# The last stage in seven tiles of 128 tokens instead of eight batches of 100, with the second attention's context re-laid by copies from DRAM to DRAM

## The reference, cut to what matters

```
x = x + L0_xattn(layernorm(x), ctx_512)      # 16 heads, causal
x = x + L0_ffn(layernorm(x))                 # 8 experts, top 2
x = x + L1_xattn(layernorm(x), ctx_512)      # 16 heads, latent context, rope
x = x + L1_ffn(layernorm(x))                 # int8-like quantised gate/up/down
```

```
ctx_c   = einsum('bhsl,bld->bhsd', attn, kv_rope)
ctx_lat = einsum('bhsd,hkd->bshk', ctx_c, w_kc_kv)
out     = ctx_lat.reshape(b, s, H * K) @ Wo.T
xq  = quant(x);  gate, up = split(xq @ quant(w_gate_up).T)
y   = quant(silu(gate) * up) @ quant(w_down).T
```

## Time and profile before

| | |
|---|---|
| median of 3 runs | 873.49 us (873.23 to 875.69) |
| the profiled execution's own time | 876.1 us |
| its span | 874.3 us |
| mean granted clock of TensorE | 0.925 |
| PE busy | 734.6 us (84%) |
| DVE busy | 522.6 us (60%) |
| ACT busy | 424.3 us (49%) |
| POOL busy | 254.4 us (29%) |
| DMA packets of the SP queue | 48605, 99.50 MB, 33.8% of 16 engines' time |

### The profile page before, as it was taken

One profiled execution on the slowest core, in us unless ns is written; L12 is line 12 of the kernel. 1 busy time (PEld: TensorE's weight loads), 2 busy tenths in 40 slices (PEclk: granted clock), 3 DMA queues, 4 the chain that ended last, 5 costly groups with the idle time before them and its releaser, 6 DMA issues.

```text
span 874.3 us, 13418 instructions
## 1 busy us (share of the span) xinstructions
PE 734.6 (84%) x4533; PEld 585.1 (67%) x4533; DVE 522.6 (60%) x1065; ACT 424.3 (49%) x790; POOL 254.4 (29%) x284
## 2 busy tenths in 40 slices
PE   0799988718999999795989989989886888999974
PEld 0597776617777777695878778778773455777752
DVE  4877675565666665255763664664663436777683
ACT  3523666255555554212664674663663314544552
POOL 1000931331122220522372461560640002222232
PEclk9997999758999999855999999999999799999997
DMA  8556632996665556952010110010015911110000
GB/s 260 189 179 220 234 105 84 351 330 230 206 212 168 181 172 203 296 116 69 1 37 23 35 46 24 22 46 24 25 39 225 339 58 48 60 57 10 10 19 19
DMA packets 51793, 108.71 MB, mean 124 GB/s; under 512 B 12149, under 2 KB 30321, under 8 KB 48953
## 3 DMA queue, kind: packets, MB, share of 16 engines
q1 hardware_dynamic: 48605, 99.50, 33.8%
q0 software_dynamic: 3136, 8.53, 4.1%
HBM read 88.59 MB, written 19.43 MB: 124 GB/s over the span
## 4 chain that ended last, share of the span: by engine, by line
PE 47%; issue 20%; DVE 12%; POOL 7%; DMA 6%; ACT 5%; SPq 1%; ACTq 1%; POOLq 0%; DVEq 0%
PE PS L148 10%; PE PS L150 9%; PE PS L149 9%; POOL wraw L759 4%; PE PS L1160 3%; PE PS L1505 3%; PE PS L1221 3%; DMA fq_raw<-foldq_in 2%; PE PS L1522 2%; ACT w_hi L811 2%; PE PS L1264 2%; DMA raw<-wkv_in 2%; DVE wscale L1760 1%; PE PS L1204 1%; DMA fp_raw<-foldp_in 1%
## 5 line engine op out<-in xcount | busy, mean ns | idle before, releaser
L759 POOL TENSOR_TENSOR wraw<-wraw,rinv 128x361 f32<-128x361 f32 (+1 forms) x104 | 80.7, 787 | 140.0 <-DVE rinv L1718 139.9
L1561 DVE TENSOR_TENSOR w_lo<-w,w_hi 128x1408 fp32r<-128x1408 f32 x40 | 64.9, 1623 | 38.6 <-ACT w_hi L811 38.6
L907 ACT ACTIVATE wraw<-PS,nmx 128x361 f32<-128x361 f32 (+1 forms) x104 | 58.6, 564 | 38.1 <-DVE nmx L1725 30.3
L1725 DVE TENSOR_REDUCE nmx<-PS 128x1 f32<-128x361 f32 (+1 forms) x104 | 55.0, 530 | 33.6 <-PE PS L150 33.6
L786 POOL TENSOR_TENSOR wraw<-gs,us 100x352 f32<-100x352 f32 x32 | 30.3, 947 | 153.4 <-ACT gs L1078 128.9
L711 POOL DMA_INDIRECT xb<-xn_scratch,rows x20 | 33.7, 1687 | 104.6 <-PE PS L1132 101.5
L811 ACT CAST w_hi<-w 128x1408 fp32r x40 | 54.7, 1369 | 16.8 <-issue 9.4
L148 PE MATMUL PS<-w_hi,xt_hi 128*128 128x352 f32 x160 | 57.0, 356 | 5.8 <-DVE xt_lo L1555 5.8
L148 PE MATMUL PS<-pf_hi,cx_hi 128*100 128x512 f32 x128 | 53.9, 421 | 8.9 <-DVE pf_lo L1896 3.7
L1728 DVE TENSOR_TENSOR pt_lo<-PS,pt_hi 128x384 fp32r<-128x384 f32 x96 | 52.3, 546 | 11.9 <-ACT pt_hi L913 11.1
L1320 PE MATMUL PS<-ident,wraw 128*128 128x128 f32 x312 | 52.0, 276 | 6.2 <-POOL wraw L759 3.4
(11 more groups left out here) (277 smaller groups left out, 2044.0 us busy)
## 6 DMA issues: line engine op xcount, KB each, us to landing
w<-w_in SPq DMA_DIRECT2D x20, 768.0 KB, 5.3
w<-w_in SPq DMA_DIRECT2D x8, 1408.0 KB, 11.5
fq_raw<-foldq_in SPq DMA_DIRECT2D x6, 1088.0 KB, 7.5
cx_raw<-ctx_scratch SPq DMA_DIRECT2D x8, 800.0 KB, 5.4
ctx_scratch<-ctxo SPq DMA_DIRECT2D x24, 256.0 KB, 2.0
ys_scratch<-yb SPq DMA_DIRECT2D x20, 256.0 KB
wraw<-wup_in SPq DMA_DIRECT2D x12, 256.0 KB, 4.4
w1q<-w_scratch SPq DMA_DIRECT2D x1, 2816.0 KB
```

The lines of the kernel that those rows point to most:

```text
L759: pool.tensor_tensor(P1[slot][0:rows, 0:NK], P1[slot][0:rows, 0:NK], rinv[0:rows, jj, t:t + 1].broadcast_to((rows, NK)), ALU.mult).then_in ...
L907: act.activation(P1[t % 8][r, 0:NK], PS[r, t % 4, 0:NK], ACT.Exp, bias=nmx[r, jj, t:t + 1], accum_out=rsum[r, jj, t:t + 1]).then_inc(C["ex ...
L1561: dve.tensor_tensor(WL[which][:, :], w12_of(dve_wlo.e, which), WH[which][:, :].bitcast(F32), ALU.subtract) \
L1725: dve.tensor_reduce(nmx[r, jj, t:t + 1], PS[r, t % 4, 0:NK], AX.X, ALU.max, negate=True).then_inc(C["max"], 1)
```

## The change

The last stage goes over NTT = 7 tiles of the 800 tokens in a row: six of 128 and one of 32. All its instructions take `tokens(n)` partitions or stationary columns in place of 100. Seven tiles need the residual and the context in that cutting:

- Residual: after the experts, SP stores X (eight DMAs of 100 rows) in `x_scratch` and loads it back in tiles (`XT`) when batch 6 of the second attention is under way. `XT` lies where X lay.
- Context: for each batch, a copy from `ctx_scratch[b]` to `tile_scratch` (DRAM to DRAM) puts the tokens in tile order. A tile's region is 128 partitions by 16 heads by tokens(n). A batch that a tile's bound cuts needs two pieces, so the eight batches are 14 pieces: 1, 2, 2, 2, 1, 2, 2, 2. Each run of contiguous bytes is one head's tokens of one piece: at most 400 bytes, and for batch 7 272 and 128. Batches 0 to 6 are copied four heads at a time, one batch later, each behind a store of the next batch; batch 7 is copied whole, after its own last store has landed.
- SP's order after that: foldp 2 and 3, load_ctx(0), foldp 4 to 7, load_ctx(1), the weights (their scale rows now for 128 partitions), load_ctx(2) and on.
- There is one buffer `CXR` in place of two: load_ctx(n) waits for `low_ctx(n - 1)`. It holds 2048 columns in place of 1600.
- The 11 transposes are split 7 and 4 over two banks in place of 6 and 5.

```
+NTT = -(-B * T // 128)
...
+        def tokens(n):
+
+            return min(128, B * T - 128 * n)
...
+        PIECES = []
+        for b in range(B):
+            cuts = sorted({b * T, (b + 1) * T} | {128 * n for n in range(NTT) if b * T < 128 * n < (b + 1) * T})
+            PIECES.append(list(zip(cuts[:-1], cuts[1:])))
...
+            for b in range(B):
+                sp.wait_ge(E["x"], TOPK * (b + 1))
+                sp.dma_start(x_scratch[b * T:(b + 1) * T], X[:, b, :]).then_inc(XSTORED, 16)
...
+            def move(b, heads, done):
+
+                h0, h1 = heads
+                for lo, hi in PIECES[b]:
+                    n = lo // 128
+                    r = tokens(n)
+                    tile = tile_scratch[:, 128 * NH0 * n:128 * NH0 * n + NH0 * r].rearrange("p (h t) -> p h t", h=NH0)
+                    batch = ctx_scratch[b].rearrange("p (h t) -> p h t", h=NH0)
+                    sp.dma_start(tile[:, h0:h1, lo - 128 * n:hi - 128 * n], batch[:, h0:h1, lo - b * T:hi - b * T]).then_inc(done, 16)
+
+            def stored(b):
+
+                sp.wait_ge(C["st0"], 16 * NG // 2 * (b + 1))
+                sp.wait_ge(C["st1"], 16 * NG // 2 * (b + 1))
+
+            for b in range(B):
+                if b + 2 < B:
+                    load_kv(b + 2, b % 2)
+                if b == B - 2:
+                    sp.wait_ge(XSTORED, 16 + 16 * B)
+                    sp.wait_ge(LN["xn"], 3 * B)
+                    full = B * T // 128
+                    sp.dma_start(XT[:, 0:full, :], x_scratch[0:128 * full].rearrange("(n p) d -> p n d", p=128)).then_inc(XLOADED, 16)
+                    sp.dma_start(XT[0:tokens(full), full, :], x_scratch[128 * full:B * T]).then_inc(XLOADED, 16)
+                if b > 0:
+                    stored(b - 1)
+                for g in range(NG):
+                    store_ctx(b, g)
+                    if b > 0:
+                        move(b - 1, (4 * g, 4 * g + 4), MOVED)
+            stored(B - 1)
+            move(B - 1, (0, NH0), MOVED_LAST)
+
+            def load_ctx(n):
+                if n == 0:
+                    sp.wait_ge(MOVED, 16 * NE + 16 * 4 * sum(len(PIECES[b]) for b in range(B - 1)))
+                if n == NTT - 2:
+                    sp.wait_ge(MOVED_LAST, 48 + 16 * len(PIECES[B - 1]))
+                wait(sp, O["cxl"], n)
+                sp.dma_start(of_tile(CXR, n), of_tile(tile_scratch[:, 128 * NH0 * n:B * ROWS], n)).then_inc(O[f"cx{n % 2}"], 16)
 
             load_foldp(2)
             load_foldp(3)
-            load_ctx(0, 0)
-            load_ctx(1, 1)
+            load_ctx(0)
             for i in range(4, NP1):
                 load_foldp(i)
+            load_ctx(1)
             sp.wait_ge(C["pv"], NG * B)
             sp.dma_start(W1Q[:, :, :], w1_scratch).then_inc(FFNW, 16)
...
+                r = tokens(n)
                 for h in heads:
-                    t = slice(h * T, (h + 1) * T)
-                    last = mm3(pe, PS[0:T, 6, :], CXH[j][:, t], CXL[j][:, t], PFH[:, h, :], PFL[:, h, :], h == 0, h == NH0 - 1)
+                    t = slice(h * r, (h + 1) * r)
+                    last = mm3(pe, PS[0:r, 6, :], CXH[j][:, t], CXL[j][:, t], PFH[:, h, :], PFL[:, h, :], h == 0, h == NH0 - 1)
...
-            for n in range(B):
+            for n in range(NTT):
                 pe_ffn(n, n % 2)
```

More of the change, by code:

```diff
@@ L321, in build_kernel @@
[L321 to L330, removed]
@@ L331, in build_kernel @@
[L331 to L333 removed]
+        S1B = sd("s1_rows", [128, 2 * FI])
+        S2B = sd("s2_rows", [128, D])
+        CXR = sd("cx_raw", [128, 128 * NH0])
+        XQ = [sd(f"xq{i}", [128, D], BF16) for i in range(2)]
+        XQT = [sd(f"xqt{i}", [128, KC, 128], BF16) for i in range(2)]
+        GS = [sd(f"gs{i}", [128, GW_]) for i in range(2)]
@@ new lines, in build_kernel, with laid_over @@
+        US = [sd(f"us{i}", [128, GW_]) for i in range(2)]
+        HQT = [sd(f"hqt{i}", [128, IC, 128], BF16) for i in range(2)]
+        pd.close()
+        def laid_over(name, shape, offset):
+            return nc.alloc_sbuf_tensor_at(name, shape, F32, offset=offset)
+        XT = laid_over("x_tiles", [128, NTT, D], X_AT)
+        Y2 = [laid_over("y2_0", [128, D], X_AT + 4 * NTT * D), laid_over("y2_1", [128, D], TABLE_AT)]
+        XNE = laid_over("xn_end", [128, 2, D], XN_AT)
+        H1 = [wraw[:, i * FI:(i + 1) * FI] for i in range(2)]
@@ new lines, in build_kernel, with smalls @@
+        HQ = [wraw[:, 2 * FI + i * FI // 2:2 * FI + (i + 1) * FI // 2].bitcast(BF16) for i in range(2)]
+        small = wraw[:, 3 * FI:3 * FI + 12 * NTT + 22]
+        def smalls(at, *dims):
+            n = int(np.prod(dims))
+            v = small[:, at:at + n]
+            return v.rearrange("p (a b) -> p a b", a=dims[0]) if len(dims) == 2 else v
+        stats_e, mv_e = smalls(0, NTT, 6), smalls(6 * NTT, NTT, 2)
+        veps_e, std_e, rstd_e = (smalls((8 + i) * NTT, NTT) for i in range(3))
@@ L658, in _ @@
[L658 to L662, removed]
+            sp.dma_start(S2B[:, :], sc_scratch[0:1, 2 * FI:2 * FI + D].broadcast_to((128, D))).then_inc(FFNW, 16)
+            for n in range(2, NTT):
+                load_ctx(n)
+            rows_out = out.rearrange("b t d -> (b t) d")
+            for n in range(NTT):
+                wait(sp, F["res"], n + 1)
+                sp.dma_start(rows_out[128 * n:128 * n + tokens(n)], XT[0:tokens(n), n, :]).then_inc(OUTS[n % 2], 16)
@@ L1504, in pe_gate_up @@
                     for k in range(KC):
-                        last = pe.matmul(PS[0:T, 2 * which + c % 2, 0:GW_], XQT[j][:, k, :], W1Q[:, k, at:at + GW_],
+                        last = pe.matmul(PS[0:tokens(m), 2 * which + c % 2, 0:GW_], XQT[j][:, k, 0:tokens(m)], W1Q[:, k, at:at + GW_],
                                          start=(k == 0), stop=(k == KC - 1))
@@ L1521, in pe_down @@
                 for c in range(IC):
-                    last = pe.matmul(PS[0:T, 7, :], HQT[j][:, c, :], W2Q[:, c, :], start=(c == 0), stop=(c == IC - 1))
+                    last = pe.matmul(PS[0:tokens(n), 7, :], HQT[j][:, c, 0:tokens(n)], W2Q[:, c, :], start=(c == 0), stop=(c == IC - 1))
                 last.then_inc(F["dn"], 1)
             def pe_ffn(n, j):
-                more = n + 3 < B
+                more = n + 3 < NTT
                 for c in range(GC - 1):
-                    if n + 1 < B:
+                    if n + 1 < NTT:
                         pe_gate_up(n + 1, 1 - j, c)
```

156 lines of the change are left out of this document (79 added, 77 removed).

## The result

| | before | after |
|---|---|---|
| median | 874.59 us (873.23 to 879.24, 4 runs) | 865.95 us (865.42 to 868.13, 4 runs) |
| profiled execution | 876.1 us | 868.13 us |
| its span | 874.3 us | 866.3 us |

The ratio is 0.9884 [0.9844, 0.9923]: the changed kernel is faster by 1.2%, 8.6 us in the medians and 8.0 us in the spans. 869.1 was forecast, with a range of 862 to 884.

What follows compares the result with a forecast made beforehand. It took TensorE (PE) to bound the last stage's steady rounds and the DMA queue the attention's end; -18.9 + 2.8 + 1.1 + 9.1 + 1.5 = -4.4 us gave a median of 869.1 us, range 862 to 884.

Steps and rivals of the forecast that it cites:

- One PE round less: Last stage: one of eight PE-bound rounds goes, -18.9 us; transposes of 128 columns in six wide tiles add +1.1 us.
- nothing is late in its place: Steady rounds: DVE's 14.45 us and the 0.5 us it gains stay under PE's 18.9 us, so no added cost.
- in steady rounds PE hides it: Steady rounds: the wider context's longer cast and subtraction, 0.94 us a pair, cost nothing behind PE's work.
- The last tile's short end: Tail: the 32-token tile shortens transposes and evictions by some tenths; counted as 0, with -1 us as bound.
- Three wider pairs: Casts and subtractions of 2048 instead of 1600 columns, three pairs on the chain at 0.94 us each: +2.8 us.
- Batch 7's copies: Attention's end: 256 packets an engine at 35 ns stand ahead of the fold loads in SP's queue: +9.1 us.
- PE's two waits for the fold loads: After the attention: PE's waits for heads 4 and 5 and heads 8 and 9 end near 681 and 686.
- The fill's late context 2: Fill: context 2 lands behind the weights, 1 to 2 us late for its ACT cast: +1.5 us (0 to 5).
- The residual through DRAM and the copies in the attention: During the attention: the residual's stores and loads and the copies of batches 0 to 6 are hidden: 0 us.
- Slow copies at 80 ns: Rival, SP's queue at 667: the copies' term is 20.6 us instead of 9.1, total 881.6 us; chance 0.23.
- The single raw buffer: Rival, fill: load_ctx(1) takes 14.9 us, PE stands 4.4 us, total 873.5 us, the gain is gone; chance 0.10.
- One more read per run (58 ns): Rival, batch 7's copies: each run brings one more read, 58 ns a packet, +5.9 us, total 875.0 us; chance 0.15.

Runs made afterwards that it cites:

- the narrow kernel: Changed kernel with the context's cast and subtraction over 1600 columns instead of 2048 in wide tiles; 861.99 us, ratio 0.9817 to the kernel before.
- the doubled copies: Changed kernel with batch 7's copies made twice, the second time into a DRAM tensor that nothing reads; 872.12 us, ratio 0.9932 to the kernel before.
- the fastest kernel: Changed kernel with batch 7's copies behind load_ctx(2), contexts 2 and 3 split earlier and the steady rounds' cast moved ahead; 852.39 us, ratio 0.9718.
- The kernel with the unused copies: Kernel before with all of the change's DRAM to DRAM copies, read by nothing, last stage still in eight batches; 883.6 us, ratio 1.0071.
- the kernel with the whole-row copy: Changed kernel with a second, unread copy of batch 7 as 128 rows of 6400 bytes; 868.51 us, ratio 0.991 to the kernel before.

## Why the prediction was right, step by step

Faster was the likeliest case at 0.42, and 866 lies between its 869.1 and its lower end of 864.5. The main step, one PE round less against a price at the attention's end, was right. But -4.4 us became -8.4 in the traces, with errors in both directions: the copies and the late context were priced 6.1 us too high, the end gave 1.5 more, and 3.6 us of the fill were not in the sum. That it came out this near is in part luck.

- **One PE round less, -18.9, with +1.1 for transposes.** Held for the round that goes. A round is 19.56 us after, which is past the 19.5 that the prediction had named as a sign of being wrong, and 19.09 where PE has no idle time: 18.9 and 0.2 for the transposes (1.1 over six tiles). The steps "nothing is late in its place" and "in steady rounds PE hides it" were right for DVE (14.28 us a round) and not for ACT: its cast of 1.9 us, in the written order, leaves PE 0.3 to 0.5 us idle. With a cast of 1.55 us or with the cast moved, rounds take 19.1. So the part with the rounds gives -17.6 (-18.9 and twice 0.65) and not -18.5.
- **The last tile's short end, 0 with -1 as its bound.** It gave -1.5, from its cast to the end.
- **Three wider pairs, +2.8.** Held, at 2.5. The cast takes 1.80 to 1.91 and the subtraction 2.20 to 2.30 instead of 1.97 and 2.33; the way from cast 0 to the projection is 0.8 longer than before, each of the two gaps in the fill 0.86, and the narrow kernel's gaps are 0.84 shorter again.
- **Batch 7's copies, +9.1.** Mis-sized, and the largest error of the sum: the first cast comes 4.9 later. 35 ns a packet was too much by 15 (20 from the doubled copies), which is 3.8 us. The wait for the landing stands (2.60 us beside 2.9 for it and batch 6). At 20 ns the same sum gives +5.3, but that this is so near 4.9 is luck too. Counted from the last store's issue, PE takes up heads 8 and 9 6.7 us later than before (at 683.99, beside 676.88), and the way from there to the cast takes 5.1 us instead of 6.9, since the fold behind it runs at a granted clock of 1.00 (684 to 688) and ran at 0.60 before (676.9 to 681). The prediction has no clock in this step. 46 ns, the two sides one after the other, is excluded.
- **PE's two waits for the fold loads.** Predicted to end near 681 and 686. The first ends at 677.78, and the second is not there: PE folds the last 12 heads without a pause (10.00 us busy of 10.00 in 678 to 688), since the later loads land while it works on heads 4 to 7 at a low clock (0.74 in the mean of 678 to 688). The first projection came at 695.5, predicted 699.5.
- **The fill's late context 2, +1.5.** This step failed: the part that holds it is -0.4, and PE waited for no context load. The issue of load_ctx(2) and the landing times of the context loads in the kernel after:

```profile
703.42 0.32 SPq L700 DMA_DIRECT2D cx_raw<-tile_scratch  x1
...
DMA to landing us min/median/max: 4.7/4.9/14.2
```

The slowest, 14.2 us, is context 2's (where it is split earlier, ACT waits until just that long after its issue). It lands at 717.6, 22.1 us after the first projection's start and not 27.5, and 4 us ahead of its cast. The prediction let the second half of the weights come at 264 GB/s; the queue moved 390 in 695.5 to 709. In the fastest kernel the cast does wait for context 2, since it is due there right behind the split of context 1.
- **A term that the sum lacks.** The fill lost +2.6 and +2.8 us elsewhere, between casts 2 and 3 and casts 3 and 4. 0.86 of each is the wider pair. The rest, 1.7 and 1.9, goes with the clock's fall behind PE's gaps (below): 0.79 over 8 us is 3.4 us at half the clock, and an estimate of what it costs is half of that, 1.7 us, each time.
- **The residual through DRAM and the copies in the attention, 0.** Held for the copies: evictions take 221 us in three kernels. The residual's loads stand in the attention of one of them, and its stores ahead of it were not tried alone. 23,600 more packets, the residual's loads among them, raised the queue's share by 16.2 points of 220 us, 24 ns of an engine's time each, near the 23 of the earlier trace rows.

**The rivals.** Slow copies at 80 ns would have put the first cast 15 us later than it came (60 ns more for each of 256 packets); the doubled copies exclude it. The single raw buffer did not starve PE in the changed kernel: ACT waits 6.8 us for context 1, and PE not at all. In the fastest kernel it holds up the chain, and PE by 0.18 us.

One more read per run (58 ns) is excluded too. The Trainium skill ("DMA: Bandwidth & Descriptors", Specifications) says that a transfer under 512 bytes is read, modified and written; the runs show what cutting costs in all, 5.1 instead of 2.9 us for 4096 runs of 272 and 128 bytes, and no run here splits these 2.2 us into descriptors and re-reading. As a size for this kernel, one more read of 23 ns a packet would have been wrong: 20 ns passed for each packet in all.

**Where much of the possible gain went.** The kernel with the unused copies shows the price, +6.2 us in ratio; the round brings about 17. Nearly all of that price is batch 7's copies (5.5 us in that kernel's trace), at a place where everything waits for the queue, and a move of two lines takes that back.

## What to carry to other kernels

Price a re-layout by where it stands in the queue, not by its packets: 24,576 packets beside the attention's work cost nothing, and 4096 behind its last store cost 6 us, though their data is wanted 100 us later. Take a packet's price from how much later a second copy lets the next work start, and not from the packets' recorded times: those overlapped and said 32 ns where 20 passed. Look at the clock before laying a shift of a few us to a transfer: in the fold it was worth 1.7 us. When a change removes work from the steady part of a pipeline, look again at its fill and its end: there the order written by hand had cost 4 us in the kernel before and 8 us in the kernel after.

## What the runs showed that was not expected

**The clock fell behind gaps that had been harmless.** The kernel before has two gaps of PE in the fill, 2.51 us to 720.08 and 1.89 us to 740.81, and a granted clock of 1.00 after both. In the kernel after they are 3.37 and 2.75 us. Windows of that kernel, 8 us from just before each gap's end:

```profile
725.00:733.00 8.00, 6.33 (x24) 4.61 (x25) 4.65 (x10) 2.46 (x4) 0.94 (x1) 0.79 0.40 131
...
749.00:757.00 8.00, 7.03 (x26) 5.02 (x27) 4.50 (x11) 3.95 (x5) 1.42 (x2) 0.79 0.38 131
```

For part of the time PE ran at the lower of its two levels, 1.2 GHz instead of 2.4. A first guess is that the longer gap is the cause, but the narrow kernel doesn't bear it out. Its gaps are as before, 2.53 and 1.92 us:

```profile
725.00:733.00 8.00, 7.10 (x22) 5.13 (x23) 3.61 (x9) 2.20 (x4) 0.94 (x1) 0.59 0.38 131
...
749.00:757.00 8.00, 7.59 (x37) 5.60 (x38) 5.97 (x15) 4.11 (x6) 1.90 (x2) 1.00 0.38 131
```

The clock fell after the first and not after the second. The kernel with the unused copies has gaps of 2.52 and 1.89 us, and its clock fell after both. In the kernel with the whole-row copy the gaps are 3.37 and 2.76 us, as in the kernel after, and the clock was 0.79 behind the first (726.8 to 734.8) and 1.00 behind the second (750.8 to 758.8). So the length of the gap doesn't decide it.

The copies don't either. In all seven profiled executions with the copies and the written order of the fill the clock fell behind the first gap, and in the one of the kernel before it did not. But where contexts 2 and 3 are split earlier, the two gaps are gone and the clock falls once in the fill, later, behind a gap of 1.96 us in three kernels; and it falls behind one of 1.66 us (0.79 in 728 to 736) in the kernel before with that edit, which has no copies. What decides it is open, with one execution of each kernel.

**SP's time for the same two copies ran from 2.4 to 13.7 us.** Batch 7's two copies with their 4096 runs keep SP for 2.4 us in the kernel after (0.54 and 1.83 us behind the landing) and 4.75 us as the second pair of the doubled copies. Where they are issued behind the weights and context 2, the same two take, in the kernel with the copies moved:

```profile
696.55 13.72 SPq L669 DMA_DIRECT2D tile_scratch<-ctx_scratch  x2
```

So the number of runs doesn't set SP's time by itself; it was longest where most stood ahead in the queue. Why is not shown.
